# Square roots of two more steps moved from ScalarE to GpSimd

## The reference

```python
def _ln(x, g, b):
    mu = jnp.mean(x, axis=-1, keepdims=True)
    var = jnp.mean(jnp.square(x - mu), axis=-1, keepdims=True)
    return (x - mu) * jax.lax.rsqrt(var + EPS) * g + b
x1 = jnp.einsum('btd,hd->bth', x, sw1) + sb1
x2 = jnp.einsum('btd,hd->bth', x, sw2) + sb2
sh = _ln(jax.nn.silu(x1) * x2, s_ln_g, s_ln_b)
shared_out = jnp.einsum('bth,dh->btd', sh, sw3) + sb3
```

## Time and profile before

| | us |
|---|---|
| median of 3 runs | 547.99 |
| lowest and highest run | 547.36, 548.27 |
| the profiled execution's own time | 548.43 |
| its span, first to last instruction | 546.3 |
| TensorE busy | 536.8 |
| VectorE busy | 396.1 |
| ScalarE busy | 264.4 |
| GpSimd busy | 167.2 |

### The profile page before, as it was taken

One profiled execution on the slowest core, in us unless ns is written; L12 is line 12 of the kernel. 1 busy time (PEld: TensorE's weight loads), 2 busy tenths in 40 slices (PEclk: granted clock), 3 DMA queues, 4 the chain that ended last, 5 costly groups with the idle time before them and its releaser, 6 DMA issues.

```text
span 546.3 us, 16500 instructions
## 1 busy us (share of the span) xinstructions
PE 536.8 (98%) x5070; PEld 480.0 (88%) x5071; DVE 396.1 (73%) x1047; ACT 264.4 (48%) x662; POOL 167.2 (31%) x527
## 2 busy tenths in 40 slices
PE   8999999999999999999999999999999999999995
PEld 5888888886899999999999999999999998875775
DVE  4979997675965757777676585887885755577686
ACT  5666757652444444244343443443433433569570
POOL 0170000000074533534435244333243230095600
PEclk9999999999999999999999999999999999999998
DMA  7831344300100002323311000000000000095234
GB/s 260 247 139 43 112 136 146 122 2 1 40 2 3 2 3 67 123 85 117 117 41 41 1 4 21 2 3 2 2 5 2 3 4 4 4 328 167 86 105 135
DMA packets 29291, 37.27 MB, mean 68 GB/s; under 512 B 5322, under 2 KB 24802, under 8 KB 28947
## 3 DMA queue, kind: packets, MB, share of 16 engines
q1 hardware_dynamic: 29106, 35.97, 20.0%
q0 software_dynamic: 96, 0.20, 0.1%
HBM read 27.69 MB, written 8.53 MB: 66 GB/s over the span
## 4 chain that ended last, share of the span: by engine, by line
PE 94%; DVE 2%; DMA 1%; issue 1%; SPq 1%; POOL 0%; ACT 0%; ACTq 0%; DVEq 0%; POOLq 0%
PE ps_out L1250 42%; PE ps_hidden L1220 41%; PE ps_hidden L628 4%; PE ps_hidden L671 2%; DMA W<-in_xT 1%; PE ps_turn L654 1%; PE ps_small L654 1%; PE ps_out L641 1%; PE ps_out L1299 1%; DVE hbuf L1446 1%; DVE hbuf L1444 1%; SPq L1034 0%; PE ps_hidden L654 0%; DVE W L1429 0%; PE ps_out L693 0%
## 5 line engine op out<-in xcount | busy, mean ns | idle before, releaser
L1250 PE MATMUL ps_out<-hbuf,W 128*128 128x242 f16 (+4 forms) x2304 | 243.0, 266 | 0.6 <-DVE W L1429 0.6
L1250 PEld LDWEIGHTS ps_out<-hbuf,W 128*128 (+1 forms) x2304 | 218.3, 98 | 17.6 <-DVE W L1429 0.9
L1876 POOL COPY xs<-X 128x88 f16 x334 | 116.5, 400 | 275.9 <-PE ps_hidden L1220 159.5
L1087 ACT ACTIVATE h<-ps_hidden,b 128x242 f32<-128x242 f32 (+3 forms) x384 | 152.1, 462 | 64.3 <-PE ps_hidden L1220 60.1
L1220 PE MATMUL ps_hidden<-xs,W 128*128 128x242 f16 (+2 forms) x1536 | 156.1, 262 | 0.4 <-issue 0.4
L1220 PEld LDWEIGHTS ps_hidden<-xs,W 128*128 (+1 forms) x1536 | 143.5, 98 | 8.2 <-issue 0.5
L1446 DVE TENSOR_TENSOR hbuf<-h,hbuf 128x484 f16<-128x484 f32 (+4 forms) x192 | 126.4, 658 | 7.5
L1739 DVE SCALAR_TENSOR_TENSOR acc<-ytmp,wrow,acc 128x44 f32 (+1 forms) x334 | 62.7, 259 | 81.9 <-ACT ytmp L1174 71.8
L1444 DVE CAST hbuf<-h 128x484 f16<-128x484 f32 (+4 forms) x192 | 83.5, 435 | 11.2 <-ACT h L1087 10.4
L1220 PE MATMUL ps_hidden<-X,W 128*128 128x256 f16 (+1 forms) x768 | 87.1, 273 | 1.6 <-DVE W L1429 1.3
L1174 ACT ACTIVATE ytmp<-ps_out,b 128x242 f32<-128x242 f32 (+3 forms) x64 | 25.5, 450 | 125.9 <-PE ps_out L1250 125.9
(11 more groups left out here) (307 smaller groups left out, 277.5 us busy)
## 6 DMA issues: line engine op xcount, KB each, us to landing
stage<-in_ew SPq DMA_DIRECT2D x16, 512.0 KB, 4.0
stage<-in_xR SPq DMA_DIRECT2D x8, 512.0 KB, 3.9
moved_rows<-stage SPq DMA_DIRECT2D x8, 512.0 KB, 2.6
X<-moved_rows SPq DMA_DIRECT2D x8, 512.0 KB, 9.5
out_rows<-X SPq DMA_DIRECT2D x16, 256.0 KB, 2.2
W<-in_xT SPq DMA_DIRECT2D x7, 512.0 KB, 9.2
W<-in_fw SPq DMA_DIRECT2D x1, 2304.0 KB, 11.0
W<-in_sw SPq DMA_DIRECT2D x4, 256.0 KB, 3.6
```

Of the source, the lines that this page charges most:

```text
L1087: i = nc.scalar.activation(h32[:, j, k * size:(k + 1) * size], ps1[j][:, k * size:(k + 1) * size], ACT.Gelu_apprx_tanh, bias=b1[:, bass.ds ...
L1250: mm = pe.matmul(out, w2(e, wp, hb, db), h, start=(n == 0), stop=(n == 3 * HB - 1))
L1876: i = nc.gpsimd.tensor_copy(xs[:, parity, :, j * SEG:(j + 1) * SEG], X[:, :, bass.ds(cols[j], SEG)])
```

## The change

GpSimd makes the reciprocal roots of steps 4 and 5 as well, in a third call, `roots(2)`, behind the gather of x. ScalarE's `root(0)` is gone and `root(1)` is now called `last_roots`; VectorE's `late_roots(2)` is gone, and `rows(4)` and `rows(5)` wait for `var_taken` instead.

```diff
-            def root(q):
-                act.wait_ge(sq_ready, 2 * q + 6)
-                two = slice((2 * q + 4) * MG, (2 * q + 6) * MG)
+            def last_roots():
+                act.wait_ge(sq_ready, NQ)
+                two = slice((NQ - 2) * MG, NQ * MG)
                 nc.scalar.activation(roots2[:, two], sums2[:, two], ACT.Sqrt, bias=epss,
                                      scale=WS * WS / FH).then_inc(root_made, 1)
...
-            root(0)
             square(NQ - 1)
             gcentre(0, 0)
             gcentre(0, 1)
-            root(1)
+            last_roots()
             gcentre(0, 2)
             groot(0)
...
-            def late_roots(q):
-                two = slice(2 * q * MG, (2 * q + 2) * MG)
-                dve.wait_ge(root_made, q - 1)
+            def late_roots():
+                two = slice((NQ - 2) * MG, NQ * MG)
+                dve.wait_ge(root_made, 1)
                 link(nc.vector.reciprocal(rstd[:, two], roots2[:, two]))
...
-                if k < 4:
+                if k < 6:
                     dve.wait_ge(var_taken, k // 2 + 1)
...
             weights(0)
-            late_roots(2)
             rows(4)
             rows(5)
             picked(0)
-            late_roots(3)
+            late_roots()
             rows(6)
...
                 x_rows(0)
+                roots(2)
                 pool.wait_ge(out_done, 16 * NH)
                 scatter(0)
```

## The result

The changed kernel takes 548.96 us (median of 19 runs, 548.25 to 550.37), the kernel before 547.79 (19 runs, 546.97 to 548.50). The ratio is 1.0026, with a 95% interval from 1.0020 to 1.0032 (the two medians alone give 1.0021): slower, by a little more than the 0.2% that I called the bound. The forecast was 549.0.

A forecast was written before the change was run, and what follows sets the result against it. TensorE sets the pace until about 540 us, then VectorE's chain leads to the end. Terms 0 + 0 + 0 + 1.08 - 0.08 = +1.00 us on 547.99 gave 549.0 us, range 548.1 to 549.9.

The forecast's parts named there:

- the bound: Whole kernel time: a difference of 0.2% (1.1 us) can just be told from no change; the forecast lay just inside.
- TensorE sets the pace, VectorE ends the kernel with 0.08 us to spare: TensorE paces until about 540 us; at the sums of j = 6 VectorE's chain has only 0.08 us to spare.
- Removing root(0) and a reciprocal brings nothing: ScalarE ahead of square(7), VectorE ahead of the rows of step 4: nobody waited for the removed work, gain 0.
- GpSimd's set is hidden, done near 521.5: Fifteen added GpSimd operations take 4.2 to 5 us, done 8 us before step 4's rows ask: cost 0.
- The load moves, rows(6) +1.08: ScalarE's 1.28 us table load lands between gcentre(0, 1)'s Square and the last roots' Sqrt, starting rows(6) 1.08 us later.
- the rival with a pause beside the load: ScalarE pauses as long again as the table load: rows(6) at +2.36, end at 550.3 us; chance 0.04.
- Sum +1.00: End of the kernel: 0 + 0 + 0 + 1.08 - 0.08 = +1.00 us, added to the median 547.99.
- TensorE's 0.39 us is hidden under VectorE's 1.08: gvariance's weight loads start 0.39 us late, but TensorE's last matmuls still end before VectorE takes j = 6.
- a sign of failure: Prediction fails if the load stands elsewhere, VectorE still waits for TensorE at the end, or step 4's rows start after 530.
- the likeliest case: Whole kernel time stays the same within the 1.1 us that can be told apart: chance 0.53, against 0.42 for slower.

The follow-up runs named there:

- dve_late: Kernel before plus one unused VectorE addition of 128x1024 between the last reciprocal and rows(6): 548.51 us, ratio 1.0012.
- after_again: The changed kernel run once more, unaltered: 548.88 us over 6 runs, ratio to the kernel before 1.0025.
- table_kept: Changed kernel plus an unused one-column square root in the place of root(0), keeping the table load ahead of square(7): 547.86 us, ratio 1.0004.
- roots_early: Changed kernel with last_roots moved right behind square(7), ahead of gcentre(0, 0), into ScalarE's idle time: 547.80 us, ratio 1.0000.
- act_pause: Kernel before plus two unused ScalarE copies ahead of gcentre(0, 2), delaying TensorE's gvariance: 549.54 us, ratio 1.0019; a second set 549.17 us, 1.0021.
- act_filled: Kernel before plus two unused ScalarE copies ahead of gcentre(0, 2) and four unused TensorE matmuls ahead of gvariance: 548.03 us, ratio 1.0012.
- filled: Changed kernel plus four unused TensorE matmuls in the idle time ahead of gvariance: 548.61 us, ratio 1.0013.

## Why the prediction was right, and where it was not

- *TensorE sets the pace, VectorE ends the kernel with 0.08 us to spare.* Right. dve_late and after_again absorb 0.10 to 0.11.
- *Removing root(0) and a reciprocal brings nothing.* Right: ScalarE's idle time grew from 0.77 to 2.34 us, the wait ahead of the rows of step 4 from 0.19 to 0.51, and both table_kept and roots_early stand at the kernel before.
- *GpSimd's set is hidden, done near 521.5.* Right: 520.11, or 521.20 with the 1.09 us between the traces. One operation took 0.65 us, the rest about 0.2.
- *The load moves, rows(6) +1.08.* Right: +1.05 to +1.06 in all three profiles, with the load starting 0.01 to 0.02 us after the Square, and the root 0.01 to 0.02 us after the load. So the rival with a pause beside the load is out. The Trainium skill ("ScalarE: Activation LUTs", What ACT_TABLE_LOAD costs) would add about 1380 ns of drain to such a switch; this trace differs, and the measurement decides.
- *Sum +1.00.* Right as the fixed part: +0.95 in two of three profiles. The medians say 548.96 - 547.79 = +1.17. That the forecast of 549.0 meets 548.96 so closely is partly luck: I added the sum to 547.99, the median of three runs, and over 19 runs it is 547.79. The start was 0.20 too high and the sum 0.17 too small.
- *TensorE's 0.39 us is hidden under VectorE's 1.08.* This is the step that failed. The 0.36 us measured are hidden in themselves, and `gsecond` was still ahead of VectorE in after_again. But I priced TensorE's late start with the durations of full clock. In some executions the clock falls to 0.50 behind it for 3.4 us, TensorE becomes the last again, and 1.08 us come on top. So in the first profile VectorE waited for TensorE near the end, which I had named as a sign of failure; in the two others it didn't. The falls fit the higher mean (+1.24), from which their share was estimated, and with them the ratio, 1.0026, landed above the bound where I had put 0.42 of the chance, and not in the likeliest case.

That ScalarE's load exposes all this is shown by roots_early and table_kept. That TensorE's idle time sets off the fall is shown as far as frequencies can show it: act_pause against act_filled, 15 of 24 long times against 1 of 11, and the changed kernel against filled, 14 of 33 above 549.0 against 1 of 11. Why the clock falls in some executions of one program and not in others isn't settled.

## What to carry to other kernels

Taking a function call from ScalarE can move a table load, since the load belongs to the first call that is left: look in the compiled order for where it lands, and put the first call with the new table into idle time, with a one-column call if need be. A short wait of TensorE in its last stage had two prices here, its length and what the work behind it cost at the lower clock (1.08 to 1.58 us in the executions with a fall); where such a wait appears, look at the granted clock behind it. When a kernel's times spread, compare stretches from one fixed event to another rather than spans, and take several profiles of the same kernel: one profile of this one showed +2.03 us and two showed +0.95.

## What the hardware showed that I had not expected

A wait of TensorE's weight loads of 0.35 us in front of 18 narrow matmuls was followed, 2.2 to 3.2 us after it had started again and while it was busy throughout, by 3.4 us at a granted clock of 0.50. In the kernel before the clock stayed at 1.00 over the same matmuls. The fall came in three of the five profiles with this wait, and in none of the seven without it, the kernel before among them. The moment of a fall isn't fixed by the program alone: behind TensorE's last matmul too, where every trace shows one, it came 2.6 us later in the kernel before (540.84 to 543.5) and 4.7 us later in after_again (540.39 to 545.1).

GpSimd's chain of 15 operations on 128x8 took 4.2 us for the second set of the kernel before, 4.6 us for the third set of the changed kernel and 7.5 us for the first set (498.34 to 505.80). The difference is in a few operations: one took 0.65 us instead of 0.20 beside VectorE's L776 (0.69 us), and two took 1.22 us beside its L765 (1.22 us).
